# Causal attention in a two-layer block: next-unit projections over three PSUM banks, with a new order on every engine

## What is computed

```python
x = L0_attn_x
xn = _layernorm(x, axis=-1)
# attention of layer 0
qkv = einsum('bse,ehd->bshd', xn, qkv_w) + qkv_b
q, k, v = split(qkv, 3, axis=-1)
logits = einsum('bqhd,bkhd->bhqk', q, k) / sqrt(64)
probs = softmax(where(tril, logits, large_negative))
attn = einsum('bhqk,bkhd->bqhd', probs, v)
x = x + einsum('bqhd,hde->bqe', attn, out_w) + out_b + ffn(xn)
```

## Time and profile before

| What | Value |
|---|---|
| median of 3 runs (range) | 1481.14 us (1479.83 to 1485.11) |
| the profiled execution, its own time | 1482.89 us |
| its span, first to last instruction | 1481.2 us |
| TensorE matmul busy | 1417.2 us, 96% |
| VectorE busy | 1255.7 us, 85% |
| GpSimd busy | 968.5 us, 65% |
| ScalarE busy | 916.9 us, 62% |
| DMA engines, mean share of the hardware queue | 47.5% |
| mean granted TensorE clock | 0.995 |

### The profile page before, as it was taken

One profiled execution on the slowest core, in us unless ns is written; L12 is line 12 of the kernel. 1 busy time (PEld: TensorE's weight loads), 2 busy tenths in 40 slices (PEclk: granted clock), 3 DMA queues, 4 the chain that ended last, 5 costly groups with the idle time before them and its releaser, 6 DMA issues.

```text
span 1481.2 us, 27229 instructions
## 1 busy us (share of the span) xinstructions
PE 1417.2 (96%) x9282; PEld 914.2 (62%) x9282; DVE 1255.7 (85%) x1966; ACT 916.9 (62%) x1862; POOL 968.5 (65%) x756
## 2 busy tenths in 40 slices
PE   8989999999999999999999998889999999999998
PEld 6755556555555565565655555456667676776767
DVE  7587888788877888888888777479999999999997
ACT  3456666666666667666666675557665675657562
POOL 5144555546555456455555554549999999999895
PEclk9999999999999999999999999999999999999999
DMA  8059777877787778777777778400000000000000
GB/s 189 1 129 217 173 172 179 185 170 175 174 185 173 172 173 186 172 168 178 181 181 166 178 177 199 102 1 1 0 9 8 1 8 1 8 8 1 8 1 15
DMA packets 77140, 163.98 MB, mean 111 GB/s; under 512 B 31410, under 2 KB 43724, under 8 KB 77004
## 3 DMA queue, kind: packets, MB, share of 16 engines
q1 hardware_dynamic: 77004, 162.24, 47.5%
HBM read 9.08 MB, written 2.10 MB: 8 GB/s over the span
## 4 chain that ended last, share of the span: by engine, by line
PE 81%; DVE 7%; issue 5%; POOL 3%; ACT 2%; SPq 0%; DMA 0%; DVEq 0%; ACTq 0%; POOLq 0%
PE accum L1095 17%; PE both L1030 12%; PE misc L997 9%; PE both L2785 8%; PE flips_all L1030 5%; PE flips_all L2808 4%; PE flips_all L1119 4%; PE misc L1007 4%; PE flips_all L2797 3%; PE flips_all L2845 2%; PE accum L2797 2%; PE accum L2808 2%; ACT big L533 2%; PE flips_all L2831 1%; PE flips_all L968 1%
## 5 line engine op out<-in xcount | busy, mean ns | idle before, releaser
L452 POOL TENSOR_SCALAR big<-big,recip 128x384 f32<-128x384 f32 (+7 forms) x512 | 374.4, 745 | 430.5 <-DVE recip L704 430.5
L712 DVE STREAM_TRANSPOSE big<-big 128x896 f32<-128x896 f32 (+7 forms) x288 | 346.0, 1227 | 17.5 <-POOL big L452 16.8
L533 ACT ACTIVATE big<-both,neg_max 128x1024 f32<-128x1024 f32 (+3 forms) x256 | 243.1, 955 | 162.7 <-DVE neg_max L694 157.5
L1095 PE MATMUL accum<-across,v_sb 128*64 128x256 f32 (+1 forms) x2560 | 272.8, 364 | 22.2 <-issue 21.8
L1095 PEld LDWEIGHTS accum<-across,v_sb 128*64 128x64 f32 x2560 | 187.0, 138 | 137.9 <-issue 82.5
L694 DVE TENSOR_REDUCE neg_max<-both 128x1 f32<-128x1024 f32 (+3 forms) x256 | 248.3, 1011 | 7.6 <-PE both L1035 7.6
L1030 PE MATMUL both<-qk_sb 64*128 64x512 f32 (+3 forms) x1024 | 212.9, 532 | 13.1 <-issue 8.2
L533 ACT ACTIVATE big<-flips_all,neg_max 128x128 f32<-128x128 f32 (+3 forms) x256 | 131.6, 525 | 102.7 <-DMA across<-big 59.8
L2785 PE MATMUL both<-slow_sb,h_T 128*128 128x512 f32 x384 | 181.2, 599 | 7.9 <-DVE xnT L2298 4.4
L1594 POOL TENSOR_TENSOR prod<-xnT,qs 128x1024 f32<-128x1024 f32 (+3 forms) x32 | 180.2, 5638 | 11.1 <-DVE qs L2298 11.1
L1030 PEld LDWEIGHTS both<-qk_sb 64*128 64x128 f32 x1024 | 94.1, 186 | 117.9 <-issue 117.9
(11 more groups left out here) (224 smaller groups left out, 2404.9 us busy)
## 6 DMA issues: line engine op xcount, KB each, us to landing
across<-big SPq DMA_DIRECT2D x1024, 144.0 KB, 3.1
out<-x SPq DMA_DIRECT2D x8, 256.0 KB, 2.3
x<-in_L_attn_x SPq DMA_DIRECT2D x3, 512.0 KB, 5.5
slow_sb<-in_L_attn_w_slow SPq DMA_DIRECT2D x3, 512.0 KB, 7.1
w_qk<-in_L_attn_qkv_w SPq DMA_DIRECT2D x2, 512.0 KB, 6.3
xn<-in_L_ffn_W SPq DMA_DIRECT2D x1, 1024.0 KB
x<-in_L_attn_x SPq DMA_DIRECT2D x2, 256.0 KB, 3.0
qs<-in_L_attn_qkv_w SPq DMA_DIRECT2D x1, 512.0 KB, 6.0
```

The lines of the kernel that those rows point to most:

```text
L452: pool.tensor_scalar(part, part, recip[:, u % 2, SLOTS.index(row), h:h + 1], 0.0, ALU.mult, ALU.add).then_inc(scaled, 1)
L533: last = act.activation(probs_of(row, h).rearrange("p b j k -> p j b k"), scores_of(row, h).rearrange("p (j b k) -> p j b k", b=MOVES, k=3 ...
L712: dve.transpose(part, part).then_inc(turned[group_of(row)], 1)
L1095: last = pe.matmul(dst, lhsT=values_of(u, j, h), rhs=keys_of(g, rows[n:n + 2], j, h), start=j == 0, stop=j == rows[n + 1])
```

## The change: what it does

The six projections of the next unit go through all three single banks in place of one, and every engine's order inside a unit is another. On VectorE, three turns of group 1 (rows 3, 2 and 4) and the inversion before them move into the next `unit`, that of row 4 behind the two maxima of the next unit's row 7; on TensorE step 5 goes ahead of the second `weigh`. SyncE's loop is bracketed otherwise, but the copies keep their sequence (group 0, group 1, unit by unit), save that the load of W1 and of W2 goes ahead of a group-0 copy where it went ahead of a group-1 copy. The numbering helper `Tally` follows. No instruction of a unit is added or removed.

```diff
-BANK = {('v', 0): 2, ('qk', 0, 1): 2, ('qk', 1, 0): 2, ('qk', 0, 0): 2, ('qk', 1, 1): 2, ('o', 0): 0, ('o', 1): 1, ('v', 1): 2}
+BANK = {('qk', 0, 1): 0, ('qk', 0, 0): 1, ('qk', 1, 1): 2, ('v', 0): 0, ('qk', 1, 0): 1, ('v', 1): 2, ('o', 0): 0, ('o', 1): 1}
+FIRST = ('v', 0), ('qk', 0, 1), ('qk', 1, 0), ('qk', 0, 0), ('qk', 1, 1), ('v', 1)
...
@@ use_of
-            return BANK[key], uses_at[BANK[key]](u, *key)
+            k = 2 if u in (0, UNITS) and key in FIRST else BANK[key]
+            return k, uses_at[k](u, *key)
@@ SyncE, loop over u
+                move(u - 1, 0)
                 move(u - 1, 1)
-                move(u, 0)
@@ GpSimd, unit(u): the order after
+                scale(u, 7, 0); scale(u, 7, 1); scale(u, 6, 1); scale(u, 1, 1); scale(u, 1, 0)
+                scale(u, 6, 0); scale(u, 2, 1); scale(u, 0, 1); scale(u, 0, 0); scale(u, 2, 0)
+                scale(u, 5, 1); scale(u, 5, 0); scale(u, 3, 0); scale(u, 3, 1); scale(u, 4, 0); scale(u, 4, 1)
                 add_part(u - 1, 0)
                 add_part(u - 1, 1)
@@ ScalarE, unit(u)
+                keep_part(u + 1, 0, 1)
                 softmax(u, 7, 1)
+                keep_part(u + 1, 0, 0)
                 softmax(u, 7, 0)
...
                 softmax(u, 0, 1)
                 softmax(u, 0, 0)
+                softmax(u, 1, 0)
                 softmax(u, 1, 1)
-                softmax(u, 1, 0)
-                keep_values(u + 1, 0)
+                softmax(u, 6, 1)
                 softmax(u, 6, 0)
-                keep_part(u + 1, 0, 1)
-                softmax(u, 6, 1)
-                keep_part(u + 1, 1, 0)
-                keep_att(u - 1, 0)
                 softmax(u, 2, 1)
                 softmax(u, 2, 0)
+                keep_att(u - 1, 0)
                 softmax(u, 5, 0)
                 softmax(u, 5, 1)
-                keep_part(u + 1, 0, 0)
-                keep_att(u - 1, 1)
                 softmax(u, 3, 0)
                 softmax(u, 3, 1)
                 keep_part(u + 1, 1, 1)
+                keep_att(u - 1, 1)
+                keep_values(u + 1, 0)
+                keep_part(u + 1, 1, 0)
+                softmax(u, 4, 1)
                 softmax(u, 4, 0)
-                softmax(u, 4, 1)
                 keep_values(u + 1, 1)
@@ VectorE, unit(u): the order after
+                invert(u - 2, 3); turn(u - 2, 3); turn(u - 2, 2)
+                maximum(u - 1, 7, 1); maximum(u - 1, 7, 0)
+                turn(u - 2, 4)
+                maximum(u - 1, 0); maximum(u - 1, 1); invert(u - 1, 0)
+                maximum(u - 1, 6, 1); maximum(u - 1, 6, 0); maximum(u - 1, 2)
+                turn(u - 1, 7); invert(u - 1, 1); invert(u - 1, 6); invert(u - 1, 4)
+                maximum(u - 1, 5, 0); maximum(u - 1, 5, 1); maximum(u - 1, 3)
+                turn(u - 1, 1); turn(u - 1, 6, 1); turn(u - 1, 0)
+                invert(u - 1, 2); invert(u - 1, 5); turn(u - 1, 6, 0)
+                maximum(u - 1, 4, 1); maximum(u - 1, 4, 0); turn(u - 1, 5)
@@ TensorE, unit(u): the order after
+                score(u, 0); project(u + 1, 0, 1); project(u + 1, 0, 0)
+                weigh(u - 1, 0, 0, 4); score_small(u, 4); score(u, 1)
+                project(u + 1, 1, 1); score_small(u, 6); weigh(u - 1, 0, 4, 8)
+                score(u, 2); score_small(u, 5); weigh(u - 1, 1, 0, 6); score(u, 3)
+                project_values(u + 1, 0); project(u + 1, 1, 0); project_values(u + 1, 1)
                 join(u - 1, 0)
                 join(u - 1, 1)
```

More of the change, by code:

```diff
@@ L122, with __init__ @@
 GROUPS = (0, 1)
-EARLY = (('qk', 0, 1), ('qk', 1, 0))
+EARLY = (('qk', 0, 1), ('qk', 1, 1))
 class Tally:
[L128 to L132, removed]
+    def __init__(self, order, head=None, tail=None, over=()):
+        self.at, n = {}, 0
+        for body in range(-1, UNITS + 2):
+            if body == -1 and head is not None:
+                keys = [(key, 1) for key in head]
+            elif body >= UNITS and tail is not None:
+                keys = [(key, -1) for key in tail]
+            else:
+                keys = order
+            for key, ahead in keys:
+                if 0 <= body + ahead < UNITS:
                     n += 1
                     self.at[(body + ahead,) + key] = n
-        self.met = 0
+            for key in over if body == UNITS - 1 else ():
+                n += 1
+                self.at[(UNITS,) + key] = n
+        self.met, self.total = 0, n
     def __call__(self, u, *key):
@@ L740, in unit @@
                     constants()
+                invert(u - 2, 3)
+                turn(u - 2, 3)
+                turn(u - 2, 2)
                 maximum(u - 1, 7, 1)
                 maximum(u - 1, 7, 0)
+                turn(u - 2, 4)
                 maximum(u - 1, 0)
@@ L766, in unit @@
                     second_sums(u - 3, GROUPS[1])
[L767 removed]
+                maximum(u - 1, 3)
+                turn(u - 1, 1)
+                turn(u - 1, 6, 1)
+                turn(u - 1, 0)
                 invert(u - 1, 2)
[L769 removed]
+                invert(u - 1, 5)
+                turn(u - 1, 6, 0)
+                maximum(u - 1, 4, 1)
                 maximum(u - 1, 4, 0)
[L771 removed]
                 if batch_over(u - 3):
                     second_variance(u - 3, GROUPS[0])
[L774 removed]
                 turn(u - 1, 5)
[L776 to L778 removed]
                 if batch_over(u - 3):
@@ L1127, in unit @@
                 score(u, 0)
+                project(u + 1, 0, 1)
+                project(u + 1, 0, 0)
+                weigh(u - 1, 0, 0, 4)
                 score_small(u, 4)
-                project_values(u + 1, 0)
-                weigh(u - 1, 0, 0, 4)
                 score(u, 1)
```

115 lines of the change are left out of this document (52 added, 63 removed).

## The result

| | before | after |
|---|---|---|
| median (range) | 1480.49 us (1478.61 to 1485.11) | 1678.72 us (1676.73 to 1681.18) |
| ratio, 95% interval | | 1.1335 [1.1304, 1.1365] |
| profiled execution, its own time | 1482.89 us | 1676.73 us |
| its span | 1481.2 us | 1675.0 us |
| TensorE busy, share | 1417.2 us, 96% | 1468.8 us, 88% |

The kernel became 13% slower. The forecast was 1636 us with a range of 1590 to 1690; the direction and the range held, and the rise was 198 us in place of 155. The forecast's own range, 1615 to 1665, did not hold: 1678.72 stands 14 us above it, in the part of the range that was kept for the clock rival (1683).

The account below looks back on a forecast made before the run. Group 1's closed round (second `weigh`, last turn, copies) was taken as the bound: 12.81 + 5.90 + 13.31 = 32.0 us against 27.01, +5.0 over 31 rounds, +155, so 1636 us; range 1590 to 1690, its own range 1615 to 1665.

Parts of the forecast that it names:

- clock rival: TensorE's new idle stretch of some 4 us lowers its clock every round: 1.5 us a round more, 1683 us; chance 0.20.
- The three banks, taken as nothing: Three banks for the projections instead of one: taken as nothing, bounds 0 and -0.2 us a round.
- Step 1 and 2: Group 1's round on TensorE: `weigh` begins 2.39 us after the landing, next unit starts at 12.81, before 10.37.
- Step 3: VectorE's turn of row 4, behind row 7's maxima, ends 5.90 us into the unit, before 3.33.
- Step 4: Group 1's set of 16 copies on SyncE's queue takes 13.31 us, no issue added.
- Group 0's landing 8.2 us into the unit: Group 0's copies land at 21.0 us after group 1's landing; TensorE wants them 4.1 into the unit, idling some 4.
- It does not lengthen the round by itself: Group 0's late landing adds nothing: work ends at 18.7 us, group 1 lands at 19.2 into the unit, cover 0.5.
- group 0 alone: Rival: group 0 has its own round of 29.2 us, +2.2, giving 1549 to 1590 us; chance 0.14, values between included.
- at most a few us: SyncE's loads of W1 and W2, each ahead of a group-0 copy once: taken as nothing, at most a few us in all.

Follow-up runs that it names:

- b_step5: Kernel before with step 5 (row 3) put ahead of the second `weigh` on TensorE: 1524.62 us, ratio 1.0287.
- b_turn_busy: b_turn plus two matmuls whose sum nobody reads, in TensorE's idle time ahead of the second `weigh`: 1552.42 us, ratio 1.0476 to the kernel before.
- b_split: Kernel before with the turn of row 4 split in two halves, each started as soon as its half is scaled: 1469.84 us, ratio 0.9913.
- a_misc: Changed kernel with all six projections in one bank again, the new orders kept: 1754.54 us, ratio 1.1822 to the kernel before.
- a_half: Changed kernel with each copy moving only half of its columns from unit 1 on, 16 issues a set as before: 1633.21 us.
- a_busy2: Changed kernel with unread matmuls ahead of the first `weigh` and of step 5, and `keep_att(u - 1, 0)` ahead of row 2's exponentials: 1662.99 us.
- b_turn: Kernel before with the turn of row 4 put behind both maxima of the next unit's row 7 on VectorE: 1600.0 us, ratio 1.0785.
- a_edges: Changed kernel with `second_deviation` back behind `scale(u, 2, 0)` and group 0's copies back ahead of the load of W2: 1661.34 us.
- a_busy: Changed kernel with three unread matmuls into `misc` ahead of the first `weigh`: 1659.42 us, ratio 1.1203 to the kernel before.

## Why the prediction was right or wrong

**What bounds the kernel before: right.** In the trace before, the second `weigh` starts 0.09 us after the last landing of group 1 in nearly every round. Three runs change the closed round of group 1 and each moves the time by what it does to the round: +1.3 us a round in b_step5 (0.4 of it by the clock), +2.3 in b_turn_busy, -0.5 in b_split. b_split takes nothing off TensorE's work, and is 12 us faster.

**The three banks, taken as nothing: right as a step from before to after**, as far as the rows go: before the change a projection waited 0.17 us a round. No run put the three banks alone into the kernel before. But the sentence was too short. Within the new orders they are worth 76 us (a_misc), the clock included. A part that is free by itself can be needed by another part of the same change.

**Step 1 and 2, unit start at 12.81: right as a sum, wrongly labelled.** I called 2.4 us "from step 5 ahead of the `weigh`". The prediction's own terms give 1.34 for that (2.39 less the 1.05 that step 5 no longer takes behind the `weigh`), and b_step5 shows 1.1 and some 0.4 of clock. The other 1.05 is the third projection, which the new order puts between the second `weigh` and the next unit. Where only the landing of group 1 holds it, the `weigh` of the changed kernel starts 2.72 us after the landing and the unit 12.69 after.

**Step 3, the turn 5.90 us into the unit: right.** Measured 5.88. By itself it costs 2.3 us a round, 2.6 forecast (b_turn_busy).

**Step 4, the copies: right.** 13.31 forecast, 13.06 measured. The figure of the Trainium skill that I had set against it (435 GB/s from SBUF to SBUF, "DMA: Bandwidth & Descriptors", section "Where 436 GB/s comes from") doesn't decide here: a_half moves half the bytes and still takes 11.84 us a set. The measured time goes mostly by issues.

**Group 0's landing 8.2 us into the unit: right** to a tenth, with 4.2 us of idle time, but partly by luck: in the unit shown the copies start 9.4 us after group 1's landing (603.39 to 612.75) and not 7.7, and the unit starts 14.1 after it and not 12.8, so that two errors nearly cancel. **"It does not lengthen the round by itself": wrong.** This is the step that failed. The cover I called thin, 0.5 us, assumed the first `weigh` at its old duration. With the clock held (a_busy2) it was nearly so: where group 0 leads, its engine work is 18.6 us, 31.5 with the copies. At the lowered clock the first `weigh` takes 4.28 or 4.96 us, by turns, instead of 2.60, and step 4, VectorE's maxima of rows 0 and 1 and all that follows stand behind it. Group 0's round behind a `weigh` of 4.96 is then 33 us, not under 32: landing 592.7, next issue 612.75, next landing 625.6. The rival "group 0 alone" had it at 29.2, in part at least because it started VectorE's chain from row 7's exponentials and left out that step 4 and the maxima of rows 0 and 1 queue behind the `weigh`. So the two rounds alternate, 31.8 and 33.

**The clock rival: its mechanism came true, beside the forecast and not in its place.** The granted clock is 0.92 over the rounds. The stretch of 4.2 us costs 1.7 or 2.4 us of matmul time in the first `weigh`, but only some 0.5 us of it a round reaches the time (32.50 against 31.97 in a_busy2), 13 us in the regular rounds and 16 by the medians, against the rival's 47. So it is luck that the result, 1679, stands next to the rival's 1683: most of the 43 us that the forecast lacked is other work, below. The Trainium skill's loop in which a DMA wait lowers the clock each turn ("TensorE: Matmul & The Clock Gate", section "HAM oscillation") is what the rounds now show: the first `weigh` takes 4.1 to 5.0 us in all 30. Where it bites depends on which idle stretch lies on the closed round: 48 us in b_turn.

**Not in the sum:** `second_deviation` on GpSimd, which the diff moves (14 us beyond the forecast for its three rounds), the load of W2, which I took "at most a few us" (6 us in the last round), and the ends (6 us). With 12 for the regular rounds these are the 39 us between 155 and the span's 194. a_edges undoes the first two and gives back 17 us, 12 of them in those four rounds. All three lie outside the regular unit from which the sum was made.

Open: why two filled gaps (a_busy2, 1659.67 to 1668.88 us) were no faster than one (a_busy, 1656.53 to 1670.42), what the three banks do alone in the old order, and whether the repairs together (edges, turn, filled gaps) would add up; they weren't tried in one kernel.

## What to carry to other kernels

When a buffer exists once and is refilled through a DMA, follow it once round (last write, copies, first read, next write allowed): that closed round can bind a kernel whose TensorE is 96% busy, and then half a microsecond on it was worth 12 us (b_split). Each group with its own buffer has its own closed round, and work queued behind one group's wait lengthens the other's; so undoing one part of a reordering can give nothing, though the part is dear alone. List the steps that run only in some units, too.

## What the hardware showed that I had not expected

- One idle stretch of 2.72 us a round before a `weigh` was enough: b_turn, with 2.6 to 3.6 us of it in its regular rounds, ran at a clock of 0.94 over them, part of the time at 1.2 in place of 2.4 GHz, where b_turn_busy, with 0.9 to 1.8 us of idle time at the same place, kept 1.00. Two matmuls that nobody reads gave back 48 us. In between it isn't the length of the stretch alone: in b_step5 the clock fell behind stretches of 1.75 and 1.80 us before step 5 and did not behind others of 2.05.
- Filling a gap can move the fall rather than end it: in a_busy it went from the first `weigh` to the second, in a third of the units.
- 16 copies out of one queue cost 0.59 to 0.63 us each to issue; a set fell only from 13.06 to 11.84 us with half the bytes.
